# Four stack pairs in place of three, an earlier load of x and another spread of the projections, in an attention and quantized-FFN kernel

## The reference, cut to what matters

```python
def proj(W):                                   # 128 x 128
    y = jnp.einsum('oc,bct->bto', W, x)
    return y.reshape(B, T, H, Dh).transpose(0, 2, 1, 3)
Q, K, V = (proj(Wq), proj(Wk), proj(Wv))
att = jnp.einsum('bhqd,bhkd->bhqk', Q, K) * (1.0 / math.sqrt(Dh)) + b[0]
att = att * m + (1.0 - m) * NEG_INF            # m: mask over the keys
y = jnp.einsum('bhqk,bhkd->bhqd', softmax(att), V)
...
h = silu(bit_linear(x, w_gate)) * bit_linear(x, w_up)
return x + bit_linear(rms_norm(h, ln_weight), w_down)
```

## Time and profile before

| what | us |
|---|---|
| median of 3 runs (lowest to highest) | 199.06 (197.01 to 200.81) |
| the profiled execution: its own time | 197.93 |
| the profiled execution: span from first to last instruction | 196.0 |
| around the span | 1.93 |
| busy PE, DVE, ACT, POOL (share of the span) | 150.5 (77%), 137.9 (70%), 133.0 (68%), 99.7 (51%) |

### The profile page before, as it was taken

How to read it: one execution, slowest core, us unless ns; L and a number is a source line. 1 busy time by engine, 2 the same in 40 slices (tenths; PEclk the granted TensorE clock), 3 DMA queues, 4 the chain that set the end, 5 groups by cost and what they waited for, 6 DMA issues and landing times.

```text
span 196.0 us, 3963 instructions
## 1 busy us (share of the span) xinstructions
PE 150.5 (77%) x1378; PEld 66.9 (34%) x1378; DVE 137.9 (70%) x205; ACT 133.0 (68%) x245; POOL 99.7 (51%) x189
## 2 busy tenths in 40 slices
PE   3783996886787896894897898898897649786783
PEld 2462543423232242331232232332323213342561
DVE  6860468676477877786988898894133968898881
ACT  3130249776698875874786977868886678999841
POOL 4898020831920831962833162064500799999940
PEclk9999999999999999999699999999999996999579
DMA  2549990237231222261231231000000000000112
GB/s 94 178 103 291 313 266 7 64 97 234 53 94 29 52 75 59 53 191 44 50 85 44 50 98 31 6 3 2 6 0 0 0 2 0 5 27 27 44 40 80
DMA packets 19915, 14.18 MB, mean 72 GB/s; under 512 B 2080, under 2 KB 19000, under 8 KB 19896
## 3 DMA queue, kind: packets, MB, share of 16 engines
q1 hardware_dynamic: 19032, 13.54, 24.5%
q10 hardware_dynamic: 864, 0.39, 0.8%
HBM read 6.17 MB, written 1.07 MB: 37 GB/s over the span
## 4 chain that ended last, share of the span: by engine, by line
PE 27%; SPq 14%; POOL 14%; DMA 13%; issue 10%; ACT 9%; DVE 9%; POOLq 1%; ACTq 0%; DVEq 0%
SPq L238 12%; PE y_ps L883 8%; POOL hw L431 7%; PE s_ps L845 7%; ACT probs L473 7%; DMA k_st<-parts 6%; DVE maxes L712 4%; PE t_ps L863 3%; POOL h_rs L442 3%; PE t_ps L821 3%; DMA q_st<-nm_rows 3%; DMA x_sb<-in_x 2%; PE t_ps L830 1%; SPq L285 1%; DMA out<-o_sb 1%
## 5 line engine op out<-in xcount | busy, mean ns | idle before, releaser
L712 DVE TENSOR_REDUCE maxes<-s_ps 128x4 f32<-128x1024 f32 x64 | 77.3, 1220 | 31.2 <-PE s_ps L845 31.1
L473 ACT ACTIVATE probs<-t_ps 128x512 f32<-128x512 f32 x128 | 71.8, 596 | 25.9 <-PE t_ps L863 25.2
L845 PE MATMUL s_ps<-k_st,q_st 64*128 64x256 bf16 x256 | 45.0, 282 | 12.8 <-DMA k_st<-parts 6.1
L863 PE MATMUL t_ps<-q_st,k_st 64*128 64x256 bf16 x256 | 44.4, 277 | 2.4 <-DMA q_st<-nm_rows 1.6
L883 PE MATMUL y_ps<-probs,v_pad 128*18 128x256 f32 x512 | 41.3, 390 | 0.1
L369 POOL TENSOR_SCALAR nm_parts<-maxes 128x16 bf16<-128x16 f32 x16 | 4.4, 275 | 62.3 <-DVE maxes L712 56.7
L845 PEld LDWEIGHTS s_ps<-k_st,q_st 64*128 64x128 bf16 x256 | 16.9, 95 | 46.9 <-issue 25.6
L431 POOL TENSOR_TENSOR hw<-hid,ln_bc 128x512 f32<-128x512 f32 x16 | 20.0, 1270 | 13.0 <-DVE hid L734 13.0
L974 PE MATMUL s_ps<-w_q,ffn_x 128*128 128x512 bf16 x64 | 17.9, 408 | 7.0 <-DVE hid L734 6.2
L863 PEld LDWEIGHTS t_ps<-q_st,k_st 64*128 64x128 bf16 x256 | 15.3, 95 | 9.5 <-ACT probs L473 5.7
L821 PE MATMUL t_ps<-x_sb,wqk_sb 128*128 128x256 f32 x28 | 11.6, 557 | 4.5 <-DMA x_sb<-in_x 3.5
(11 more groups left out here) (95 smaller groups left out, 219.3 us busy)
## 6 DMA issues: line engine op xcount, KB each, us to landing
q_st<-parts SPq DMA_DIRECT2D x48, 64.0 KB
k_st<-parts SPq DMA_DIRECT2D x42, 64.0 KB
w_f<-in_wgT SPq DMA_DIRECT2D x1, 1024.0 KB, 8.4
w_f<-in_wuT SPq DMA_DIRECT2D x1, 1024.0 KB, 5.0
w_f<-in_wdT SPq DMA_DIRECT2D x1, 1024.0 KB, 6.0
out<-o_sb SPq DMA_DIRECT2D x8, 128.0 KB, 1.7
x_sb<-in_x SPq DMA_DIRECT2D x1, 640.0 KB, 4.5
mask_bc<-in_cond SPq DMA_DIRECT2D x1, 640.0 KB, 5.7
```

The source lines that it names most:

```text
L473: act.activation(probs[:, t % NP_RING].rearrange("p e t -> p (e t)"), src, ACT.Exp, scale=SCALE)\
L712: dve.tensor_reduce(dst[:, :, s, :], s_ps[:, c % 2], AX.X, ALU.max).then_inc(s_maxed, 1)
L845: mm = pe.matmul(s_ps[:, c % 2, i, e, :], q_st[b % 3][rows, hp, qt * P:qt * P + P], k_st[b % 3][rows, hp, :], start=True, stop=True)
L863: mm = pe.matmul(t_ps[:, u % 2, e, :], k_st[b % 3][rows, hp, kt * P:kt * P + P], q_st[b % 3][rows, hp, :], start=True, stop=True)
```

## The change

The tables of slots change, a constant `RING = 4` takes the place of 3 in everything that indexes or counts stacks, the x load of batches 3 to 7 is issued ahead of batch 0's stack and its mask load stays behind, the load of the first masks goes behind the V weights, and the bias store goes ahead of the low parts of Q of batch 0. The scratch tile `w_junk` goes; the sums of weights write their unused output to `hid_sq`, which the attention doesn't use.

```diff
-QK_SLOTS = {(-1, 0): 3, (-1, 2): 4, (-1, 4): 5, (-1, 7): 6, (0, 7): 7}
-V_SLOTS = {(-1, 1): 3, (-1, 3): 4, (-1, 5): 5, (0, 1): 6, (0, 3): 7}
+QK_SLOTS = {(-1, 0): 3, (-1, 3): 4, (0, 0): 5, (0, 4): 6, (0, 7): 7}
+V_SLOTS = {(-1, 1): 1, (-1, 4): 2, (0, 1): 3, (0, 3): 4, (0, 5): 5, (1, 0): 6, (1, 1): 7}
...
-EARLY = (("qk", 1), ("v", 0), ("qk", 2), ("v", 1), ("v", 2))
+EARLY = (("qk", 1), ("v", 0), ("qk", 2))
...
+RING = 4
...
-        k_st = [sb(f"k_st{r}", [P, NHP, T], bf16) for r in range(3)]
-        q_st = [sb(f"q_st{r}", [P, NHP, T], bf16) for r in range(3)]
+        k_st = [sb(f"k_st{r}", [P, NHP, T], bf16) for r in range(RING)]
+        q_st = [sb(f"q_st{r}", [P, NHP, T], bf16) for r in range(RING)]
...
-        w_junk = sb("w_junk", [P, 1024], f32)
...
             def load_rows(b):
-                if b < 3:
+                if b < RING:
...
-                    sp.wait_ge(unit_ready, unit["t", 16 * (b - 2) - 1] + 1)
-                    sp.dma_start(q_st[b % 3][MAX_ROWS], zeros6[:, :, :].to_broadcast([6, NHP, T]))\
-                      .then_inc(stack_in[b % 3], 16)
+                    sp.wait_ge(unit_ready, unit["t", 16 * (b - RING + 1) - 1] + 1)
+                    sp.dma_start(q_st[b % RING][MAX_ROWS], zeros6[:, :, :].to_broadcast([6, NHP, T]))\
+                      .then_inc(stack_in[b % RING], 16)
...
-            sp.dma_start(x_sb[:, 0, :], x[0]).then_inc(x_in[0], 16)
+            load_x(0)
...
-            sp.dma_start(mask_bc[:, 0, :], cond[0].partition_broadcast(P)).then_inc(mask_bc_in[0], 16)
-            load_inputs(1)
+            load_mask(0)
+            load_x(1)
             sp.dma_start(wv_sb[:, :], wvT).then_inc(wv_in, 16)
+            load_mask(1)
+            load_x(2)
             load_rows(0)
             load_high(0, 0)
-            load_low(0, (0,))
             sp.wait_ge(bias_step, 7)
             sp.dma_start(bias_scr, bias_parts[:, :, :, :].to_broadcast([B, 2, 3, T])).then_inc(bias_stored, 16)
+            load_low(0, (0,))
             load_bias(0)
-            load_inputs(2)
+            load_mask(2)
             load_weights(0)
...
-            for r in range(1, 3):
+            for r in range(1, RING):
                 clear_stacks(r)
...
             project_qk(1)
             project_v(0)
             project_qk(2)
-            project_v(1)
-            project_v(2)
```

More of the change, by code:

```diff
@@ L174, in adaln_ffn_kernel @@
         bias_stored = sem("bias_stored")
-        stack_in = [sem(f"stack_in{r}") for r in range(3)]
+        stack_in = [sem(f"stack_in{r}") for r in range(RING)]
         nm_in = [sem(f"nm_in{r}") for r in range(2)]
@@ L233, in load_part @@
         def load_part(queue, b, side, part):
-            stack = (q_st, k_st)[side][b % 3]
+            stack = (q_st, k_st)[side][b % RING]
             for slot in range(len(SPLITS)):
                 if SPLITS[slot][side] == part:
-                    queue.dma_start(stack[slot::SLOTS], parts[:, b % 2, side, part, :]).then_inc(stack_in[b % 3], 16)
+                    queue.dma_start(stack[slot::SLOTS], parts[:, b % 2, side, part, :]).then_inc(stack_in[b % RING], 16)
         block = ctx.enter_context(nc.Block())
@@ L243, in _, with load_x, load_mask @@
         def _(sp):
-            def load_inputs(r):
+            def load_x(r):
                 b0, b1 = GROUPS[r], GROUPS[r + 1]
                 sp.dma_start(x_sb[:, b0:b1, :], x[b0:b1].rearrange("b c t -> c b t")).then_inc(x_in[r], 16)
+            def load_mask(r):
+                b0, b1 = GROUPS[r], GROUPS[r + 1]
                 sp.dma_start(mask_bc[:, b0:b1, :].rearrange("p b t -> p (b t)"),
@@ L266, in load_bias @@
                     sp.wait_ge(bias_stored, 16)
-                sp.dma_start(k_st[b % 3][BIAS_ROWS],
+                sp.dma_start(k_st[b % RING][BIAS_ROWS],
                              bias_scr[b].rearrange("i k t -> (i k) t").unsqueeze(1).to_broadcast([6, NHP, T]))\
-                  .then_inc(stack_in[b % 3], 16)
+                  .then_inc(stack_in[b % RING], 16)
             def load_high(b, side):
@@ L284, in load_max_rows @@
                 sp.wait_ge(unit_free, unit["rows", g] + 1)
-                sp.dma_start(q_st[b % 3][MAX_ROWS, 4 * tau:4 * tau + 4, :], nm_rows[:, g % 2, :])\
+                sp.dma_start(q_st[b % RING][MAX_ROWS, 4 * tau:4 * tau + 4, :], nm_rows[:, g % 2, :])\
                   .then_inc(nm_in[g % 2], 16)
@@ L524, in sum_weights @@
                     act.wait_ge(abs_done, q)
-                act.activation(w_junk[:, :], w_f[:, m, 1024 * part:1024 * part + 1024], ACT.Abs,
+                act.activation(hid_sq[:, :], w_f[:, m, 1024 * part:1024 * part + 1024], ACT.Abs,
                                accum_out=w_abs[:, q:q + 1]).then_inc(abs_done, 1)
@@ L839, in scores @@
                     if k == 0:
-                        pe.wait_ge(stack_in[b % 3], 16 * LOADS * (b // 3 + 1))
+                        pe.wait_ge(stack_in[b % RING], 16 * LOADS * (b // RING + 1))
                     if c >= 2:
@@ L844, in scores @@
                 rows = slice(64 * i, 64 * i + 64)
-                mm = pe.matmul(s_ps[:, c % 2, i, e, :], q_st[b % 3][rows, hp, qt * P:qt * P + P],
-                               k_st[b % 3][rows, hp, :], start=True, stop=True)
+                mm = pe.matmul(s_ps[:, c % 2, i, e, :], q_st[b % RING][rows, hp, qt * P:qt * P + P],
+                               k_st[b % RING][rows, hp, :], start=True, stop=True)
                 if i == 1 and e == 1:
@@ L862, in scores_t @@
                 rows = slice(64 * i, 64 * i + 64)
-                mm = pe.matmul(t_ps[:, u % 2, e, :], k_st[b % 3][rows, hp, kt * P:kt * P + P],
-                               q_st[b % 3][rows, hp, :], start=True, stop=True)
+                mm = pe.matmul(t_ps[:, u % 2, e, :], k_st[b % RING][rows, hp, kt * P:kt * P + P],
+                               q_st[b % RING][rows, hp, :], start=True, stop=True)
                 if e == 1:
```

8 lines of the change are left out of this document (3 added, 5 removed).

## The result

| | before | after |
|---|---|---|
| median of 20 runs each (lowest to highest), us | 198.84 (195.9 to 202.18) | 199.24 (197.43 to 202.33) |
| profiled execution: own time; span | 197.93; 196.0 | 198.82; 197.0 |
| mean granted TensorE clock in the span, as the profile prints it | 0.964 | 0.939 |

The ratio of after to before is 1.0091, 95% interval 1.0050 to 1.0132: the change costs some 1.8 us (0.91% of 199), where 5.3 us were forecast as gained. The time lies above the range given. Ratios leave disturbed runs out, so a ratio can differ a little from that of two medians.

A forecast was written before the change was run, and what follows sets the result against it. No engine was at its limit; a ring of hand-overs between TensorE, DVE and ACT set each stage unless loads came late. 3.5 - 3.3 + 1.4 + 4.2 - 0.5 = 5.3 us gained: 193.7 us, range 190.0 to 197.8.

The forecast's parts named there:

- Part 1: At the start, bias store and x load go earlier, so the first exponential comes earlier than 34.43: 3.5 us gained.
- at the old distance of 2.27 us: At the start, the bias store, issued at 9.3 or before, lands 2.27 us later, by about 11.5.
- at 22.8 + 5.0 = 27.9: In stage -1, the second weight matrix, 5.0 us in landing, arrives at 27.9; ACT's third and fourth sums wait for it.
- The rival that weights gate the start: At the start, the second weights land no earlier; the start gains 1.5 us, the sum 3.3, time 195.7; chance 0.15.
- Part 2: Stages 0 and 1 receive one qk and three V projections more, at 1.2 and 0.7 us each: 3.3 us lost.
- the rival that gives 4.8: In stages 0 and 1, each moved projection costs what a qk does, 4.8 us; sum 3.8, time 195.2; chance 0.10.
- Part 3: At the end of stage 0, the max-row load is nearly in time as the third weights have more lead: 1.4 us gained.
- Part 4: At the borders of stages 3 to 6, the fourth stack pair frees SP and stack stalls shrink: 4.2 us gained.
- 92.04 - 2.60 - 76.95 = 12.49: Stage 3 of the kernel before, less its stack stall of 2.60 us, taken as a plain stage of 12.49 us.
- 1.08 over the plain one: Stage 4 without its stall took 13.57 us, 1.08 over a plain stage, partly at the lower clock; that goes.
- Part 5: Around the start of stage 0, TensorE waits some 2 us for ACT and its clock may drop: 0.5 us lost.
- the clock stays down: TensorE stays at 1.2 GHz through stages 0 and 1, some 29 us, costing 9.5 us, not 0.5: 202.8; chance 0.08.

The follow-up runs named there:

- the clock held up: The changed kernel with three useless matmuls more behind each step of stage -1 from k = 1 and behind the first of stage 0; ratio to before 1.0020.
- the experiment: The changed kernel with the x load of batches 3 to 7 issued behind the bias store, still ahead of the bias load; ratio to before 1.0083.
- the third weights late: Four pairs, new load order, old slots, third weights issued behind batch 1's first max rows: ratio to before 0.9866; with extra matmuls too, 0.9865.

## Why the prediction was wrong, by its own steps

**Part 1, the start, failed: 3.5 us forecast, 0.5 in the trace, 1.9 with the clock held up.** Two steps were wrong. The store was to land "at the old distance of 2.27 us"; with 640 KB of x issued ahead of it in the same queue, the bias load could go 4.95 us behind the store, and the first scores came at 16.04. The prediction had cited the Trainium skill (DMA: Bandwidth & Descriptors, "Queues, rings and completion order") as speaking "against x ahead of the stack of batch 0", and worked out no price. What the store waits for is the landing of x, 7.2 us from issue in after's page; the trace agrees with the rule, by the 4.95 and by the 4.64 of the experiment. The second wrong step is the weights: "at 22.8 + 5.0 = 27.9". They were issued at 25.16, later than before, since the queue ahead of them carried the same issues and now a later bias load, and landed at about 30.3. (The quoted sum is 27.8, a slip of 0.1.) The rival that weights gate the start was right on this.

**Part 2, the units, failed in its price: 3.3 forecast, 4.3 at full clock.** The steps are read from the run with extra matmuls against the earlier trace rows: qk of 6 2.73 - 1.14 = 1.6, V of 5 2.31 - 1.53 = 0.8, V of 6 2.31 - 1.14 = 1.2, V of 7 0.8. The prediction took V at 0.7 and qk at 1.2 from units that stood alone. Behind a lone unit the next reduction follows at once (a step of 1.14, "x2" in the earlier trace rows), and a part of the delay comes back. With a unit in the next step too, as at k = 3, 4 and 5 in the new tables, nothing comes back. The run with two of them taken back bears it out: from the first exponential to the first maxima of batch 2 it takes 14.4 us in place of 17.0, 2.6 less, for 2.4 by these steps and 1.9 by the prediction's. Of that 0.7 is lost again ahead of the first exponential (33.19 for 32.50), where the two units now stand. This is close to the rival that gives 4.8.

**Part 3, the max rows, was right: 1.4.** The wait is gone in after, and the runs with the third weights late show that the weights ahead in the queue caused it. But taking it away in another kernel (0.9866 beside 0.9840) bought nothing that could be measured, while with the extra matmuls the kernel without the wait was 3.4 us faster (0.9865 beside 1.0037), more than the wait itself.

**Part 4, the fourth pair, failed in its size: 4.2 forecast, 2.1 in the change and 0.9 alone, neither clear of nothing.** The mechanism was as told. In after SP issues the second max rows within 0.1 us of their copies, and the stalls are 0.97, 0.89, 0.30 and 0.37 us, where about 0.3, 1.6, 1.0 and 0 were forecast. Wrong was to read a shorter stall as a shorter stage, with "92.04 - 2.60 - 76.95 = 12.49" as the plain stage. After's rows around a small stall:

```profile
107.36 0.27 PE L848 MATMUL s_ps<-k_st,q_st 64*128 64x256 bf16 x1 [0.30 <-DMA k_st<-parts]
...
109.11 0.28 PE L848 MATMUL s_ps<-k_st,q_st 64*128 64x256 bf16 x1 [0.47 <-DVE maxes L715]
```

Where the stack comes in time, TensorE waits for DVE two steps later, since DVE carries a backlog of maxima over the border; in a longer stall DVE works that off, so a part of the stall is not lost. Before, behind the stall of 0.98 us at the same border, that wait was 0.16 us (at 109.18), so 0.3 of the 0.7 us by which the stall shrank came back there; where the rest went is not read. The four stages of after from batch 3's first maxima on last 13.2 to 13.5 us with stalls under 1 us; none was near 12.5. Moreover the profile before had two long stages (15.2 and 14.4 us by first maxima); in the profiles of order alone and slots alone, with three pairs and about 5 us of stalls, the same two last 13.5 to 13.9, and without the ring in the change 15.0 and 13.5. The "1.08 over the plain one" of the clock hung on one profile.

**Part 5, the clock, failed in size: 0.5 forecast, 2.9 in the traces, 1.4 by the ratios.** After and the run with the clock held up differ by some 19 us at the lower level. At the first maxima of batch 2 they are 4.0 us apart (53.49 and 49.47), 0.2 a us of low clock; 1.0 of it the second run loses in stage 2, by a drop of its own (14.4 us for 13.4). The rival "the clock stays down" took 0.33 a us for 29 us. It had the place right, stage 0. Its cause, an emptier stage -1 ahead of dense ones, is not shown: in all four profiles with the old slots and the new order, and no extra matmuls, the clock fell too, between 31 and 37 us, for 6.8 us. What is new in after, and in the run with three pairs, is only that it fell for 13.7. The Trainium skill (TensorE: Matmul & The Clock Gate, "HAM oscillation") describes a kernel whose short matmul bursts each start at the lower clock, because the waits between them are long. The trace agrees only in part: here the clock fell behind a stretch in which TensorE was busy for 2.75 of 3.90 us (25.6 to 29.5) with no idle piece over 0.94, and it came back after 13.7 us of which TensorE was busy for some 12.

**The sum again.** From 5.3: less 1.6 at the start (first exponential at 32.5 with the clock up, not 30.9), less 1.0 for the units, less 2.4 for the clock, less 2.1 for the ring, gives -1.8, the measured ratio's. That they meet is luck in good part: each term is known to about 1 us, traces and ratios are mixed, and with the ratios' 1.4 us for the clock the sum would be -0.3.

**What stays open.** Why the clock is lost in some profiles and kept in others at the same place isn't settled; it differs even between kernels whose code is the same up to there. Ring and order had it low from 31.2 to 38.0; with the third weights late, the same code up to 41 us, it was low up to 28.7 and from 35.6 to 42.4. Nor is it shown why the order gains 2.3 us with the old slots though its first exponential is hardly earlier (33.99 for 34.43): at the first maxima of batch 4 its profile is still 0.7 us behind that of before (79.00 for 78.26), and it gets ahead only in the two stages that were long before.

## What to carry to other kernels

Read the price of moved work at a place whose neighbours are like the ones it will have, as work standing alone is partly won back in the step behind it, and never take a stage less its stall for the plain stage: look which engine had a backlog. Before a large load is put ahead in a queue, list the small transfers behind it that gate something, and charge them its landing. The low stretches of TensorE's clock move from profile to profile of the same code, so compare several profiles before one stage's length is taken as given.

## What the runs showed of the hardware

**Small transfers behind a large one.** With the 640 KB of x ahead of it, the 24 KB bias store took so long that its load could go 4.95 us behind it, in place of 2.27; with x between the two, the load itself took 4.64 us, and the first scores came 4.68 us behind its issue (12.36 to 17.04), where it was 2.21 before (13.10 to 15.31).

**More work, less time.** With three matmuls more in each step of a half-empty stage the granted clock stayed at 1.00 where it had been 0.51, and the attention ended 2.9 us sooner. In a fuller stage the same matmuls brought nothing, or cost 3.9 us.

**The clock is not set by the code alone.** Two kernels with the same instructions up to 42.5 us had TensorE at the lower level from 13.7 to 20.6 and from 34.2 to 41.1 in the one profile, and from 13.4 to 33.9 in the other.

**A drop behind the attention costs time too.** Two kernels with the same slots, clocks apart. First the one without extra matmuls, then the one with them:

```profile
131.90:141.00 9.10, 7.83 (x73) 2.66 (x68) 1.95 (x4) 6.38 (x14) 4.77 (x7) 0.81 0.02 4
```

```profile
129.10:138.20 9.10, 7.61 (x80) 2.62 (x72) 2.03 (x4) 7.51 (x16) 4.77 (x7) 1.00 0.02 4
```

From the start of the last reduction to the end of the span the first takes 65.1 us and the second 62.3, with the same instructions. Some 1.1 us of the 2.8 go with the drop: the run of after's slots with the clock held up has a drop at the same place and takes 63.4. The other 1.7 are something else, a last wait of DVE for an output store that landed in 3.7 us in place of 1.7:

```profile
DVE o_sb L771 <- DMA out<-o_sb: 2.5, 1, 2.5
```

Together they are more than the whole effect of the change, in a part of the kernel that the change doesn't touch. The runs of one kernel spread over some 6 us; such drops and waits are likely causes of it, though not shown to be.
